# Linear attention's denominator: a masked block matmul replaced by two rounded passes over q_phi scaled by the key sums

## The reference

```python
def layer(h, p):                       # h: (8, 512, 128), 16 heads of 8
    q = _phi((h @ wq + bq_).reshape(b, s, H, DH))     # _phi(t) = elu(t) + 1
    k = _phi((h @ wk + bk_).reshape(b, s, H, DH))
    v = (h @ wv + bv_).reshape(b, s, H, DH)
    kv = jnp.einsum('bshd,bshm->bhdm', k, v)
    z = 1.0 / (jnp.einsum('bshd,bhd->bsh', q, k.sum(axis=1)) + 1e-06)
    att = jnp.einsum('bshd,bhdm,bsh->bshm', q, kv, z).reshape(b, s, d)
    h = _ln(h + att @ wo + bo_, g1_, be1_)
    y = jax.nn.gelu(h @ w1 + c1_, approximate=False) @ w2 + c2_
    return (_ln(h + y, g2_, be2_), None)
...
x = x + s * g          # s: eight layers and a last norm; g: silu of the expert branch
```

## Time and profile before

| | |
|---|---|
| median of 3 runs | 957.02 us (956.54 to 958.22) |
| the profiled execution | 954.39 us |
| its span, first to last instruction | 952.7 us |
| granted TensorE clock, mean over the span | 0.972 of full speed |
| PE busy | 872.2 us, 92% |
| DVE busy | 764.7 us, 80% |
| ACT busy | 694.9 us, 73% |
| POOL busy | 275.9 us, 29% |

### The profile page before, as it was taken

One profiled execution on the slowest core, in us unless ns is written; L12 is line 12 of the kernel. 1 busy time (PEld: TensorE's weight loads), 2 busy tenths in 40 slices (PEclk: granted clock), 3 DMA queues, 4 the chain that ended last, 5 costly groups with the idle time before them and its releaser, 6 DMA issues.

```text
span 952.7 us, 18936 instructions
## 1 busy us (share of the span) xinstructions
PE 872.2 (92%) x5782; PEld 744.7 (78%) x5782; DVE 764.7 (80%) x2722; ACT 694.9 (73%) x1077; POOL 275.9 (29%) x302
## 2 busy tenths in 40 slices
PE   3649999999999999999999999999999999997880
PEld 1538888888888888888888888888888888876650
DVE  6786778887788778788788879777888778889777
ACT  2447788787888787877878887878778788876450
POOL 6003222232322222321233122422223232245442
PEclk9769999999999999999999999999999999999995
DMA  4101020001000000001000100001000000000002
GB/s 156 59 1 22 3 40 1 21 2 40 2 18 2 31 8 1 19 0 39 1 20 0 39 1 0 19 0 39 1 20 0 0 1 1 1 2 0 1 1 88
DMA packets 22440, 16.67 MB, mean 17 GB/s; under 512 B 3964, under 2 KB 18280, under 8 KB 22376
## 3 DMA queue, kind: packets, MB, share of 16 engines
q1 hardware_dynamic: 22376, 16.00, 5.7%
HBM read 13.89 MB, written 2.10 MB: 17 GB/s over the span
## 4 chain that ended last, share of the span: by engine, by line
PE 78%; DVE 14%; issue 4%; ACT 2%; DMA 0%; DVEq 0%; POOL 0%; POOLq 0%; ACTq 0%
PE down_ps L654 21%; PE q_ps L604 6%; PE small_ps L593 5%; PE att_ps L623 5%; PE q_ps L586 5%; PE k_ps L580 5%; PE up_ps L648 4%; PE up_ps L646 4%; PE up_ps L647 4%; PE t_ps L630 3%; PE t_ps L570 3%; DVE st L829 2%; PE small_ps L598 2%; PE att_ps L612 1%; PE small_ps L607 1%
## 5 line engine op out<-in xcount | busy, mean ns | idle before, releaser
L654 PEld LDWEIGHTS down_ps<-w_use,hid 128*128 128x128 f32 x2048 | 249.6, 192 | 30.1 <-issue 30.0
L654 PE MATMUL down_ps<-w_use,hid 128*128 128x128 f32 x2048 | 260.5, 276 | 0.0
L870 POOL TENSOR_TENSOR res_att<-z_tm,g_att 128x512 f32<-128x512 f32 x64 | 81.5, 1274 | 475.5 <-DVE mv L835 475.4
L726 ACT ACTIVATE hid<-up_ps 128x512 f32<-128x512 f32 x192 | 114.9, 599 | 25.6 <-PE up_ps L648 9.9
L829 DVE BATCH_NORM_STATS2 st<-h 128x6 f32<-128x128 f32 x512 | 105.5, 279 | 2.2
L751 ACT ACTIVATE den<-q_ps,den_eps_col 128x512 f32<-128x512 f32 x64 | 44.0, 687 | 67.1 <-PE q_ps L604 67.1
L792 ACT ACT_TABLE_LOAD x64 | 82.1, 1283 | 1.1
L910 DVE TENSOR_TENSOR blk<-small_ps,head_mask 128x256 f32<-128x256 f32 x64 | 27.1, 423 | 69.4 <-PE small_ps L599 69.4
L804 ACT ACT_TABLE_LOAD x63 | 80.8, 1283 | 1.1
L877 POOL TENSOR_TENSOR res_ffn<-z_tm,g_ffn 128x512 f32<-128x512 f32 x64 | 81.2, 1269 | 0.0
L646 PE MATMUL up_ps<-z_hi,w_hi 128*128 128x512 f32 x192 | 81.0, 422 | 0.3 <-DVE gate_bc L490 0.3
(11 more groups left out here) (180 smaller groups left out, 1782.1 us busy)
## 6 DMA issues: line engine op xcount, KB each, us to landing
raw_w<-in_L_attn_W SPq DMA_DIRECT2D x16, 256.0 KB, 4.5
x_tm<-in_L_attn_x SPq DMA_DIRECT2D x4, 512.0 KB, 5.8
bias_bc<-in_L_attn_c SPq DMA_DIRECT2D x8, 256.0 KB, 4.2
out_y<-gate_tm SPq DMA_DIRECT2D x8, 256.0 KB, 2.0
raw_g<-in_L_attn_g SPq DMA_DIRECT2D x15, 64.0 KB
raw_att<-in_L_attn_Wq SPq DMA_DIRECT2D x8, 64.0 KB, 1.8
raw_att<-in_L_attn_Wk SPq DMA_DIRECT2D x8, 64.0 KB, 2.0
raw_att<-in_L_attn_Wv SPq DMA_DIRECT2D x8, 64.0 KB, 1.9
```

The source lines that it names most:

```text
L654: last = nc.tensor.matmul(down_ps[:, t, :], hid[:, j, t * P:(t + 1) * P], w2_use[:, j, :], start=False, stop=(j == FC - 1 and t == TT - 1))
L726: nc.scalar.activation(hid[:, j, :], up_bank[j], ACT.Gelu).then_inc(s["gelu"], 1)
```

## The change

The masked key-sum block is gone. The key sums become one column (`ks_col`), so the matmul that makes them has one output column, and it is moved ahead of the key-value matmul. The head mask itself, whose zeros and ones are exact in fp32r, becomes the weights of the denominator. The moving operand is q_phi times the key sums, split in two: ScalarE writes the product rounded to fp32r (`prod_hi`), VectorE writes what the rounding left (`prod_lo`), and TensorE accumulates a pass over each. ScalarE's Relu of k now stands in a function of its own, with prod_hi between it and k's Exp. On VectorE prod_lo stands behind the z1 norms. On TensorE the denominator moves behind the second group of the down projection, and the third group stands between the z1 transposes and q. GpSimd makes one more constant at the start. No DMA changes.

```diff
@@ -49,6 +49,7 @@
         mean_f32 = sb("mean_f32", [P, P])
         ones = sb("ones", [P, P])
         ones_r = sb("ones_r", [P, P], F32R)
+        head_mask_r = sb("head_mask_r", [P, P], F32R)
         row_sel = sb("row_sel", [2, 1])
         eps_col = sb("eps_col", [P, 1])
         den_eps_col = sb("den_eps_col", [P, 1])
@@ -105,7 +106,11 @@
         q_e = sb("q_e", [P, S])
         q_phi = sb("q_phi", [P, S])
         g_sb = sb("g_sb", [P, P])
-        blk = sb("blk", [P, 2, P])
+        blk = sb("blk", [P, P])
+        ks_col = sb("ks_col", [P, 1])
+
+        prod_hi = sb("prod_hi", [P, S], F32R)
+        prod_lo = sb("prod_lo", [P, S], F32R)
         kvo = sb("kvo", [P, P])
         den = sb("den", [P, S])
         rden = sb("rden", [P, S])
@@ -129,7 +134,7 @@
         q_ps = ps("q_ps", [P, S])
         k_ps = ps("k_ps", [P, TT, D])
         small_ps = ps("small_ps", [P, 4, P])
-        G_PS, KV_PS, KVO_PS = small_ps[:, 0, :], small_ps[:, 1:3, :], small_ps[:, 3, :]
+        G_PS, KV_PS, KS_PS, KVO_PS = small_ps[:, 0, :], small_ps[:, 1, :], small_ps[:, 2, 0:1], small_ps[:, 3, :]
         up_ps = [ps(f"up_ps{i}", [P, S]) for i in range(2)]
         down_ps = ps("down_ps", [P, TT, D])
         att_ps = ps("att_ps", [P, TT, D])
@@ -595,16 +600,18 @@
 
         def pe_kv_ksum(pe, u):
             pe.wait_ge(s["g_sb_s"], u + 1)
-            nc.tensor.matmul(KV_PS[:, 0, :], w_v[:, :], g_sb[:, :], start=True, stop=True)
-            nc.tensor.matmul(KV_PS[:, 1, :], g_sb[:, :], mean_f32[:, :], start=True, stop=True).then_inc(s["kv_ps_s"], 1)
+            nc.tensor.matmul(KS_PS, g_sb[:, :], mean_f32[:, 0:1], start=True, stop=True)
+            nc.tensor.matmul(KV_PS, w_v[:, :], g_sb[:, :], start=True, stop=True).then_inc(s["kv_ps_s"], 1)
 
         def pe_den(pe, u):
+            pe.wait_ge(s["prod_hi_s"], u + 1)
+            nc.tensor.matmul(q_ps[:, :], head_mask_r[:, :], prod_hi[:, :], start=True, stop=False)
+            pe.wait_ge(s["prod_lo_s"], u + 1)
+            nc.tensor.matmul(q_ps[:, :], head_mask_r[:, :], prod_lo[:, :], start=False, stop=True).then_inc(s["den_ps"], 1)
+
+        def pe_kvo(pe, u):
             pe.wait_ge(s["blk_s"], u + 1)
-            pe.wait_ge(s["qphi"], u + 1)
-            nc.tensor.matmul(q_ps[:, :], blk[:, 1, :], q_phi[:, :], start=True, stop=True).then_inc(s["den_ps"], 1)
-
-        def pe_kvo(pe, u):
-            nc.tensor.matmul(KVO_PS, blk[:, 0, :], w_o[:, :], start=True, stop=True).then_inc(s["kvo_ps_s"], 1)
+            nc.tensor.matmul(KVO_PS, blk[:, :], w_o[:, :], start=True, stop=True).then_inc(s["kvo_ps_s"], 1)
 
         def pe_att_bias(pe, u):
             if after_first(u):
@@ -691,22 +698,25 @@
             if ffn:
                 pe_down(pe, p - 2, (0,))
             if att:
-                pe_den(pe, p)
                 pe_kvo(pe, p)
             if between:
                 between()
             if ffn:
                 pe_down(pe, p - 2, (1,))
+            if att:
+                pe_den(pe, p)
             if ln1:
                 if b == 4 and is_layer(l + 1):
                     pe.wait_ge(s["fold_a"], l + 2)
                 if b == 5 and is_layer(l + 1):
                     pe.wait_ge(s["fold_f"], l + 2)
                 pe_z1_transpose(pe, p - 1, p + 2 if state or not isinstance(p, int) else UNITS)
+            if ffn:
+                pe_down(pe, p - 2, (2,))
             if proj:
                 pe_q(pe, p + 1, b + 1)
             if ffn:
-                pe_down(pe, p - 2, (2, 3))
+                pe_down(pe, p - 2, (3,))
             if att:
                 pe_att(pe, p)
             if state:
@@ -754,13 +764,22 @@
                 act.wait_ge(s["qn"], p)
             nc.scalar.activation(rden[:, :], den[:, :], ACT.Exp, scale=-1.0).then_inc(s["rden_s"], 1)
 
-        def act_k_exp(act, u):
+        def act_k_relu(act, u):
             act.wait_ge(s["kproj"], u + 1)
             if after_first(u):
                 act.wait_ge(s["kphi"], u)
             nc.scalar.activation(k_e[:, :, :], k_ps[:, :, :], ACT.Relu, scale=-1.0, bias=ones[:, 0:1]).then_inc(s["krel"], 1)
+
+        def act_k_exp(act, u):
             act.wait_ge(s["krel"], u + 1)
             nc.scalar.activation(k_e[:, :, :], k_e[:, :, :], ACT.Exp, scale=-1.0).then_inc(s["kexp"], 1)
+
+        def act_prod_hi(act, u):
+            act.wait_ge(s["ks_s"], u + 1)
+            act.wait_ge(s["qphi"], u + 1)
+            if after_first(u):
+                act.wait_ge(s["prod_lo_s"], u)
+            nc.scalar.activation(prod_hi[:, :], q_phi[:, :], ACT.Identity, scale=ks_col[:, 0:1]).then_inc(s["prod_hi_s"], 1)
 
         def act_q_exp(act, u):
             act.wait_ge(s["qproj"], u + 1)
@@ -792,6 +811,10 @@
                 nc.scalar.preload_act_table_set("natural_log_exp_and_others")
             if ln1 or ln2 or fin:
                 act_rstd(act, p, ln1, ln2, fin)
+            if proj:
+                act_k_relu(act, p + 1)
+            if att:
+                act_prod_hi(act, p)
             if proj:
                 act_k_exp(act, p + 1)
             if att:
@@ -907,8 +930,13 @@
 
         def dve_blocks(dve, u):
             dve.wait_ge(s["kv_ps_s"], u + 1)
-            nc.vector.tensor_tensor(blk[:, :, :], KV_PS, head_mask[:, :].unsqueeze(1).to_broadcast([P, 2, P]),
-                                    ALU.mult).then_inc(s["blk_s"], 1)
+            nc.vector.tensor_copy(ks_col[:, :], KS_PS).then_inc(s["ks_s"], 1)
+            nc.vector.tensor_tensor(blk[:, :], KV_PS, head_mask[:, :], ALU.mult).then_inc(s["blk_s"], 1)
+
+        def dve_prod_lo(dve, u):
+            dve.wait_ge(s["prod_hi_s"], u + 1)
+            nc.vector.scalar_tensor_tensor(prod_lo[:, :], q_phi[:, :], ks_col[:, 0:1], prod_hi[:, :].bitcast(F32),
+                                           ALU.mult, ALU.subtract).then_inc(s["prod_lo_s"], 1)
 
         def dve_kvo(dve, u):
             dve.wait_ge(s["kvo_ps_s"], u + 1)
@@ -1000,6 +1028,8 @@
                 dve_shift(dve, p, ln1, ln2, fin)
             if ln1:
                 dve_norm1(dve, p, p - 1)
+            if att:
+                dve_prod_lo(dve, p)
             if proj:
                 dve_k_phi(dve, p + 1)
             if att:
...
```

More of the change, by code:

```diff
@@ L146, in build @@
             t2_ps zfm kproj krel kexp tk kphi qproj qrel qexp tq qphi
-            g_ps_s g_sb_s kv_ps_s blk_s kvo_ps_s kvo_sb den_ps den_sb rden_s qn
+            g_ps_s g_sb_s kv_ps_s ks_s prod_hi_s prod_lo_s blk_s kvo_ps_s kvo_sb den_ps den_sb rden_s qn
             t2m t1m att_done h1_s st1_s mv1_s h2_s st2_s mv2_s st3_s mv3_s lnv_s rstd_s mr_s shift_s
@@ L324, in build @@
         gate_bc = sb("gate_bc", [P, SEQS])
-        CONSTS = 16
+        CONSTS = 17
         STATS_GROUPS = [(i, i + 2) for i in range(0, SEQS, 2)]
@@ L1097, in _ @@
                 nc.gpsimd.memset(zeros[:, :], 0.0).then_inc(c, 1)
-                pool.wait_ge(c, 14)
+                nc.gpsimd.tensor_copy(head_mask_r[:, :], head_mask[:, :]).then_inc(c, 1)
+                pool.wait_ge(c, 15)
                 nc.gpsimd.tensor_copy(row_att[:, :, :], zeros[:, :].unsqueeze(1).to_broadcast([P, TT, D])).then_inc(c, 1)
```

## The result

The changed kernel takes 1011.62 us (median; 1008.84 to 1012.46 in 4 runs) against 956.78 us for the kernel before in the same comparison: 1.057 times the time, interval 1.054 to 1.060. The forecast was 999.6 us, the range 972 to 1018.

What follows compares the result with a forecast made beforehand. TensorE's row of slots was taken to bound the kernel, 12.75 us per period. Costs by place in the layer summed to 42.6 us on the profiled 954.39, giving 997.0, or 999.6 us against the median; range 972 to 1018.

Steps and rivals of the forecast that it cites:

- the saving: TensorE slots: denominator as two fp32r passes, minus 0.40 us, and shorter key sums, minus 0.04; 0.44 us per unit.
- the key-sum term: TensorE's key-sum pair with one output column instead of 128: 0.18 us instead of 0.22, minus 0.04 per unit.
- The wait for prod_lo: TensorE's second denominator pass waits for VectorE's prod_lo, 0.51 us late; net +0.06 us per unit.
- GpSimd's hold on m_r: VectorE's m_r waits for GpSimd's second product to end, 0.30 us later than alone; ordinary period 13.09 against 12.75, +0.34.
- the ring: Period loop: prod_lo, denominator, Ln, rden, q_n, VectorE's row, GpSimd's products, m_r, norms, next prod_lo at T+13.09 us.
- the four terms that I added up to 1.98: From prod_lo's end to q_n: pass start 0.16, pass 0.40, Ln 0.69, rden 0.63 us; claimed T+1.98.
- rival A: The wait for prod_lo alone costs, m_r coming after GpSimd's product: 28 us more, 985 us; chance 0.28.
- ScalarE at nothing: ScalarE's added prod_hi, 0.63 us between k's Relu and Exp, ends by R+1.5 before VectorE reaches prod_lo; costed at nothing.
- The last five units: Final norms also on VectorE there, prod_lo adds its 0.6 us to each: 3 us in all.
- The start: First two units, with VectorE's start-up work between blocks and norms: 1 us each, 2 in all.
- B: Rival: prod_lo is ready before TensorE reaches the second pass, so the saving comes through: 27 us less, 930; chance 0.07.
- C: Rival: prod_lo or prod_hi costs more than its row, prod_lo 1.27 instead of 0.69 us: 31 more, 1030; chance 0.14.

Runs made afterwards that it cites:

- the swapped kernel: Changed kernel with GpSimd's two residual products in the other order, res_ffn ahead of res_att: 994.91 us, ratio 1.039.
- no-wait kernel: Changed kernel with both denominator passes reading prod_hi, prod_lo still computed but not waited for: 957.98 us; with GpSimd's products also in the other order 947.22 us.
- the one experiment on it: Changed kernel with prod_lo put ahead of VectorE's start-up work in units 0 and 1 only: 1008.87 us, ratio 1.057.
- the kernels with prod_lo early: Changed kernel with prod_lo directly behind the blocks, prod_hi ahead of k's Relu, z1 transposes behind the third down group: 990.61 us; three further reorderings 982.78, 974.55, 974.69.

## Why the prediction was right, and where its sizes were off

- **TensorE is the bound and the saving is real: right.** 12.38 against 12.75 without the wait, 0.37 of the 0.44 I had. Of the missing 0.07, 0.04 is the key-sum term, which is zero. The floor that the Trainium skill gives ("TensorE: Matmul & The Clock Gate", "Wait — 56ns, not 53.3ns?"), by which I estimated 0.17, is not reached here, where 128-column weights are loaded for each matmul: 0.44 us with 1 or 128 columns.
- **The wait for prod_lo takes the saving's place: right in kind, a little too small.** prod_lo takes 0.745 us, not 0.69. With the hold gone (the swapped kernel) the period is 12.96, 0.58 above the same slots without a wait, where my terms gave 0.50; together with the missing 0.07 that makes +0.21 over before, where +0.06 was the forecast.
- **GpSimd's hold on m_r, inside the ring: right.** m_r 0.33, ending 0.03 behind the product; 13.13 to 13.19 in units with b=7, forecast 13.09. The ring came out step by step: from the end of prod_lo at 361.38, q_n starts 1.98 later, res_att 8.60, the two products end 11.09 and m_r 11.11; the forecasts were 1.98, 8.6, 11.1 and 11.12. One slip is in it: the four terms that I added up to 1.98 make 1.88, and it is the total that fits. The swap gave back 16.7 us; 14.6 us lay between the forecast and rival A for it. In the no-wait kernel, where TensorE does not wait for prod_lo and the ring is open, the hold was still worth 10.8, and 6.5 in the kernel before, nearly all of it in b=1 and the last units. The rule of the Trainium skill ("SBUF — State Buffer", "Who interferes with whom") agrees in both directions here: m_r, with both inputs in SBUF, is held for the rest of GpSimd's instruction, and is not once the two do not meet. aff_att has one input, and is of the kind that the page lets into the two-port mode; it was held too.
- **"ScalarE at nothing": right where prod_lo is late,** since prod_hi ends at 359.70, 0.93 before prod_lo starts. It failed at once when prod_lo was moved early: 0.59 us of waiting for prod_hi per unit.
- **By place:** what follows the blocks of a b shows in the next b's distance. fold_att +0.69 against 0.5, fold_w1 +0.81 against 0.65, the spread norms +0.85 against 0.8, the loop turn +1.29 against 1.9, the split of W1 +1.21 against 0.9, the three ordinary ones (b=2, 3, 7) +1.38 against 1.02. The split was right only in that it costs: I had the cast held for longer, and it is held for less; it is the subtraction behind it that is held. That the errors of the loop turn and the split partly cancel is luck. The sum is 6.2 per layer against 5.8; over the six layers 36.1 against 33.1.
- **The last five units: mis-sized,** 6.4 against 3.0. I counted prod_lo's 0.6 alone. From block product to q_n it is 5.09 us in units 60 to 62, where it was 3.14, 3.71 and 3.96, so what is late is more than prod_lo. m_r takes 0.89 there; it took 0.21 in unit 60, but was already held in units 61 and 62 (0.83). The swap alone brought the periods of units 61 and 62 from 17.1 to 16.4.
- **The start: mis-sized,** 6.1 against 2.0, and the one experiment on it failed. Its cause stays open. 1.7 us of it lie ahead of the first block product, where the granted clock was 0.80 instead of 1.00. In the experiment's run it was 1.00 there, so no run shows these 1.7 us as a cost of the change.

The rivals: A (985) is the swapped kernel in all but name, 994.9, so its mechanism is 10 us dearer than I made it; some 5 of them are aff_att's new hold in b=4, which A did not have. B needed an open ring; with the ring open by leaving out the remainder, it still came to 958, not 930, because the places outside the ordinary units give nothing. C's price, 1.27 for prod_lo, did not occur (0.725 to 0.778).

What stays open, beside the start: whether a version that leaves the denominator at its old place could keep the saving in b=0 as well. It wasn't tried. An estimate from the rows: the old place comes 0.69 us behind the block product's start (R+1.00 less R+0.31), 359.52 in the period shown, and prod_hi ends at 359.70, so the first pass would wait 0.2 us there, and the second for prod_lo. Open is also why the clock falls earlier in the drain of the kernels with prod_lo early.

## What to carry to other kernels

Before trading TensorE time for a pass on another engine, find the ring that the result travels, here block product, prod_lo, denominator, q_n, residual products, m_r: slack is to be read at its tightest period (the loop turn, the folds), not from the 80% of the page. A saving in the engine that bounds the ordinary units counts only in those units, and putting an operation later to make room for its new inputs has a price of its own (here 0.64 of the 1.41 us by which q_n came later). Where two GpSimd products have different readiness, try first the one that is ready first, and look at what it then meets on VectorE (here aff_att). And read a loss by stretches, with the granted clock of each, before putting it down to the order of instructions.

## What was unexpected of the hardware

- A pair of 1-column f32 matmuls with 128-column weights buys nothing: 0.44 us to the slot after next with 1 or 128 columns.
- SCALAR_TENSOR_TENSOR with all operands in SBUF, 128x512 with an fp32r result, takes 0.745 us (0.725 to 0.778); TENSOR_TENSOR of that size takes 0.69, and the folds with one operand in PSUM 0.68.
- An operation as small as 128x8 was held until the end of a 1.27 us GpSimd instruction: up to 1.03 us for 0.16 of work. So was a 128x128 TENSOR_SCALAR with a single tensor input, 1.41 us for 0.35.
- At 1.2 GHz a pair of 128x512 f32 matmuls took 1.97 us instead of 1.07. With 56 matmuls left when the clock fell, the stretch behind the last block product was 75.6 us instead of 69.5 (mean granted clock 0.70 instead of 0.82).
